# Turning the rows of x and of the softmax shift with DMA transposes in a fused attention kernel

## The reference

```python
xn = _layernorm(x)
# attention on xn
q = (layernorm(xn) * norm_g + norm_b) @ Wq;  k, v = split(xn @ Wkv)
q = q / max(|q|, 1e-12) * q_scale;           k = k / max(|k|, 1e-12) * k_scale
sim  = q @ k.T * 8 - slope[h] * |i - j|      # causal, two null keys ahead
out  = softmax(sim) @ v;                     out = out @ Wout
# result
x + out + ffn(xn)                            # ends in layernorm(...) * ln_g + ln_b
```

## Time and profile before

| | us |
|---|---|
| time, median of 3 runs | 3170.33 |
| lowest, highest | 3167.26, 3171.96 |
| the profiled execution, its own time | 3174.85 |
| its span, first to last instruction | 3173.0 |
| PE busy | 2914.2 |
| DVE busy | 2680.4 |
| ACT busy | 2252.6 |
| POOL busy | 2248.3 |

### The profile page before, as it was taken

The page is one execution under the profiler, slowest core; times in us unless marked ns, Lnnn a source line. Parts: engine busy times, 40 slices in busy tenths (PEclk is TensorE's granted clock), DMA queues, the critical chain, the costliest instruction groups (busy, mean ns, idle before and its releaser), DMA issues.

```text
span 3173.0 us, 86275 instructions
## 1 busy us (share of the span) xinstructions
PE 2914.2 (92%) x32783; PEld 1729.7 (55%) x32783; DVE 2680.4 (84%) x6642; ACT 2252.6 (71%) x3572; POOL 2248.3 (71%) x2588
## 2 busy tenths in 40 slices
PE   4589999899998999989998999989999899998998
PEld 4245555555555556555555555555555555555555
DVE  6778888888888888888888888888888888888887
ACT  3467777676866777767776677766777676867776
POOL 5876677867778577876778668786677867778663
PEclk8799999999999999999999999999999999999999
DMA  3111221212121121211212122121211212221111
GB/s 115 44 25 25 58 42 48 55 22 58 45 64 35 32 58 35 71 28 40 57 40 66 22 50 53 42 58 25 58 42 48 55 22 58 45 64 35 25 25 38
DMA packets 320329, 144.72 MB, mean 46 GB/s; under 512 B 284336, under 2 KB 286384, under 8 KB 319920
## 3 DMA queue, kind: packets, MB, share of 16 engines
q1 hardware_dynamic: 318448, 139.12, 18.5%
q10 hardware_dynamic: 1472, 0.09, 0.0%
HBM read 55.23 MB, written 16.78 MB: 23 GB/s over the span
## 4 chain that ended last, share of the span: by engine, by line
PE 60%; DVE 22%; issue 9%; POOL 7%; ACT 2%; DVEq 0%; POOLq 0%; ACTq 0%
PE PS L1262 8%; PE PS L1237 8%; PE PS L1241 7%; PE PS L1240 7%; DVE PS L1032 7%; PE PS L1285 4%; PE PS L1310 3%; DVE QKB L1047 3%; DVE AR L1070 3%; PE PS L1312 3%; PE PS L1314 3%; PE PS L1331 3%; PE PS L1333 3%; PE PS L1332 3%; PE PS L1266 2%
## 5 line engine op out<-in xcount | busy, mean ns | idle before, releaser
L1032 DVE CUSTOM_DVE_ANT_0 PS<-PS,STR 128x512 f32<-128x512 f32 (+3 forms) x1536 | 825.4, 579 | 192.1 <-PE PS L1285 190.7
L573 ACT ACTIVATE AR<-PS,SC 128x1024 f32<-128x1024 f32 (+1 forms) x640 | 658.5, 1029 | 418.5 <-PE PS L1293 250.0
L1237 PE MATMUL PS<-WH,XT 128*128 128x388 f16 x2048 | 684.4, 334 | 57.7 <-DVE AR L1039 48.4
L799 POOL TENSOR_TENSOR RN<-SS,HALF 128x8 f32<-128x8 f32 x256 | 436.4, 1705 | 417.3 <-DVE SS L1118 412.9
L1240 PE MATMUL PS<-WL,XT 128*128 128x388 f16 x2048 | 684.1, 334 | 0.0
L1241 PE MATMUL PS<-WH,XT 128*128 128x388 f16 x2048 | 683.9, 334 | 0.0
L577 ACT ACTIVATE AR<-AR 128x1024 f16<-128x1024 f32 (+1 forms) x640 | 621.7, 971 | 20.3
L1070 DVE TENSOR_TENSOR AR<-AR 128x768 f16<-128x768 f32 (+1 forms) x448 | 516.3, 1167 | 11.8 <-ACT AR L577 11.8
L1262 PE MATMUL PS<-AR 64*128 64x512 f16 (+3 forms) x4608 | 504.7, 328 | 3.9 <-ACT AR L573 3.8
L1310 PE MATMUL PS<-AR 128*128 128x66 f16 x4608 | 478.0, 193 | 3.9 <-DVE AR L1070 3.8
L1312 PE MATMUL PS<-AR 128*128 128x64 f16 x4608 | 477.7, 195 | 0.0
(11 more groups left out here) (247 smaller groups left out, 5803.6 us busy)
## 6 DMA issues: line engine op xcount, KB each, us to landing
XW<-in_L_attn_x SPq DMA_DIRECT2D x112, 256.0 KB, 2.7
out<-ACC SPq DMA_DIRECT2D x64, 256.0 KB, 2.1
ACC<-in_L_attn_x SPq DMA_DIRECT2D x56, 256.0 KB, 2.7
AR<-QKB SPq DMA_TRANSPOSE x512, 2.5
AR<-in_L_attn_Wkv SPq DMA_DIRECT2D x2, 1536.0 KB, 13.9
ACC<-in_L_attn_x SPq DMA_DIRECT2D x2, 1024.0 KB, 7.1
AR<-in_L_attn_Wout SPq DMA_DIRECT2D x1, 2048.0 KB, 8.4
AR<-in_L_attn_Wq SPq DMA_DIRECT2D x2, 512.0 KB, 5.3
```

Of the source, the lines that this page charges most:

```text
L573: e.activation(PR[:, n % 2, :, 0:wide], SB[:, :, 0:wide], ACT.Exp, scale=SIG).then_inc(s_p, 1)
L799: e.tensor_tensor(RN[:, i % 2, :], SS[:, i % 2, :], HALF[:, :], ALU.pow).then_inc(s_rn, 1)
L1032: e.tensor_tensor_reduce(out=r[:, 0:n], in0=r[:, 0:n], in1=ST[:, u % 2, h, o:o + n], scale=1.0, scalar=LOW, op0=ALU.add, op1=ALU.max, accu ...
L1237: e.matmul(PJ, XT[:, k, xs], WH[:, k, p, :], start=k == 0, stop=False)
```

## The change

1. Rows of x: `ln_tp` on PE and `ln_out` on ACT are gone. SP issues one DMA transpose per row tile, `turn_rows`, from `XHL` straight into `XT`: 128 rows by 1024 numbers. Each of the two slots has its own semaphore. Ahead of the loop the 8 turns of batch 0 stand in SP's queue behind the loads.
2. Rows with the shift: the four turns on PE and the copy on ACT are gone. SP issues one DMA transpose of 128 rows by 512 numbers per half unit.
3. Neither takes a bank of the ring any more.
4. Keys and queries: the factor `KA` is moved into the norm. DVE scales the sum of squares by 1/(KA*KA) in the instruction that takes the larger one, ACT copies without a scale, and DVE makes the low part of a group with one plain subtraction of 128 by 512 instead of two scaled ones of 128 by 256. SP waits for the whole group before it turns either tile.
5. All tables are new.

```diff
-W_PIECE = [45, 46, 50, 56, 62, 66, 71, 74, 78, 82, 84, 90]
-W_SCORE = [90, 94, 98, 104, 108, 113, 118, 122, 126, 132]
+W_PIECE = [45, 46, 48, 57, 64, 66, 70, 74, 77, 82, 84, 91]
+W_SCORE = [91, 94, 100, 105, 108, 114, 118, 122, 126, 132]
...
-W_PROJ = [z for z in [0, 6, 12, 23, 28, 32, 40, 44] for k in range(KC)]
-W_TP = [29, 34, 56, 66]
-W_LO = [26, 38, 48, 61]
-W_SHIFT = [70, 91]
-W_CTP = [75, 96]
-W_CT = [75, 95]
+W_PROJ = [z for z in [-1, 7, 12, 23, 28, 32, 40, 43] for k in range(KC)]
+W_TP = [36, 45, 56, 69]
+W_LO = [27, 39, 56, 65]
+W_SHIFT = [69, 91]
+W_CTP = [75, 99]
...
-W_XL = [-36, -31, -24, -5, 1, 2, 14, 22]
-W_XTP = [-28, -28, -12, -8, 5, 7, 18, 34]
-W_XT = [-30, -28, -13, -10, 5, 13, 19, 38]
+W_XL = [-36, -36, -26, -8, -5, 9, 29, 34]
+W_XTP = [-33, -30, -22, 4, 10, 20, 22, 41]
...
-HOLD = [4.6, 5.2, 6.1, 6.2, 6.8, -39.0, 6.5]
+HOLD = [4.6, 5.2, 7.1, -60.5, 5.5]
...
+            def turn_rows(b, t):
+                w.wait_ge(s_xl, NT * b + t + 1)
+                if b:
+                    w.wait_ge(s_proj, (NP * b - 1) * NT + t + 1)
+                e.dma_start_transpose(XT[:, :, P * t:P * t + P], XHL[:, t % 2, :, :].rearrange("p j c -> p (j c)")).then_inc(s_xt[t % 2], 16)
+            for t in range(NT):
+                turn_rows(0, t)
...
+                for u, qc in due(s, W_CTP):
+                    w.wait_ge(s_c, 2 * u + qc + 1)
+                    w.wait_ge(s_cz, 2 * (2 * u + qc) + 2)
+                    if u > 1:
+                        w.wait_ge(s_st, 2 * NS * (u - 1))
+                    e.dma_start_transpose(CT[:, u % 2, 512 * qc:512 * qc + 512].rearrange("p (q n) -> p q n", q=4),
+                                          CTK[:, qc, :, :].rearrange("p q r -> p (q r)")).then_inc(s_ct[qc], 16)
+                for b, t in due_ln(s, W_XTP):
+                    turn_rows(b, t)
                 for u, g in due(s, W_TP):
...
+                    w.wait_ge(s_lo, i + 1)
                     for t in range(2):
                         c = 256 * g + P * t
-                        w.wait_ge(s_lo, 2 * i + t + 1)
...
-                                 SQ2[:, i % 2, :].rearrange("p (t j c) -> p t j c", t=2, c=64), ACT.Copy, scale=KA).then_inc(s_hi, 1)
+                                 SQ2[:, i % 2, :].rearrange("p (t j c) -> p t j c", t=2, c=64), ACT.Copy).then_inc(s_hi, 1)
...
-                    for t in range(2):
-                        e.scalar_tensor_tensor(
-                            out=QKH[:, i % 3, t, 256:512].rearrange("p (j c) -> p j c", c=64),
-                            in0=SQ2[:, i % 2, 256 * t:256 * t + 256].rearrange("p (j c) -> p j c", c=64), scalar=KA,
-                            in1=QKH[:, i % 3, t, 0:256].rearrange("p (j c) -> p j c", c=64), op0=ALU.mult,
-                            op1=ALU.subtract).then_inc(s_lo, 1)
+                    e.tensor_tensor(QKH[:, i % 3, :, 256:512], SQ2[:, i % 2, :].rearrange("p (t c) -> p t c", t=2),
+                                    QKH[:, i % 3, :, 0:256], ALU.subtract).then_inc(s_lo, 1)
...
-                    e.tensor_tensor(SS[:, i % 2, :], SS[:, i % 2, :],
-                                    CL[:, u // NP % 2, 2 * g:2 * g + 2, :].rearrange("p t c -> p (t c)"), ALU.max).then_inc(s_ss, 1)
+                    e.scalar_tensor_tensor(out=SS[:, i % 2, :], in0=SS[:, i % 2, :], scalar=1.0 / (KA * KA),
+                                           in1=CL[:, u // NP % 2, 2 * g:2 * g + 2, :].rearrange("p t c -> p (t c)"),
+                                           op0=ALU.mult, op1=ALU.max).then_inc(s_ss, 1)
```

More of the change, by code:

```diff
@@ L143, in take @@
         last[i], read[i] = who, slot
-    for t in range(NT):
-        take(t - 600, "xt", 0, t)
     for s in SLOTS:
@@ L152, in ring_order @@
             take(s + HOLD[2], "op", u, t)
[L153 to L156, removed]
         for u, qc in due(s, W_NTP):
-            take(s + HOLD[5], "nt", u, qc)
+            take(s + HOLD[3], "nt", u, qc)
         for u, qc in due(s, W_OTP):
-            take(s + HOLD[6], "otp", u, qc)
+            take(s + HOLD[4], "otp", u, qc)
     return at, before
@@ L343, in bank_free @@
             what, u, i = BEFORE[who]
-            if what == "xt":
-                e.wait_ge(s_xt, NT * u + i + 1)
-            elif what == "s":
+            if what == "s":
                 e.wait_ge(s_mx, 24 * u + i + 1)
@@ L349, in bank_free @@
                 e.wait_ge(s_add, NT * (u // 2) + i + 1)
-            elif what == "ct":
-                e.wait_ge(s_ct, 2 * u + i + 1)
             elif what == "nt":
@@ L542, in _ @@
                     e.activation(QKH[:, i % 3, :, 0:256].rearrange("p t (j c) -> p t j c", c=64),
-                                 SQ2[:, i % 2, :].rearrange("p (t j c) -> p t j c", t=2, c=64), ACT.Copy, scale=KA).then_inc(s_hi, 1)
-                for u, qc in due(s, W_CT):
-                    w.wait_ge(s_ctp, 2 * u + qc + 1)
-                    if u > 1:
-                        w.wait_ge(s_st, 2 * NS * (u - 1))
-                    else:
-                        w.wait_ge(s_spl, 20)
-                    e.activation(CT[:, u % 2, 512 * qc:512 * qc + 512], rb("ct", u, qc).bitcast(F16)[:, 0:512],
-                                 ACT.Copy).then_inc(s_ct, 1)
+                                 SQ2[:, i % 2, :].rearrange("p (t j c) -> p t j c", t=2, c=64), ACT.Copy).then_inc(s_hi, 1)
                 for u, qc in due(s, W_NT):
@@ L1199, in _ @@
                     bias(j // 2)
-            def ln_tp(b, t):
-                r = rb("xt", b, t).bitcast(F16)
-                bank_free(w, "xt", b, t)
-                w.wait_ge(s_xl, NT * b + t + 1)
-                for j in range(8):
-                    ins = e.transpose(r[:, P * j:P * j + P], XHL[:, t % 2, j, :], IDH[:, :])
-                ins.then_inc(s_xtp, 1)
             null_columns(NP - 1)
@@ L1213, in _ @@
             ins.then_inc(s_bqn, 1)
-            for t in range(NT):
-                if t == 6:
-                    w.wait_ge(s_am, 1)
-                    e.transpose(PS[0:8, 2, 192:320], AM[:, 0:8], IDF[:, :]).then_inc(s_amt, 1)
-                    w.wait_ge(s_dg, 1)
-                    e.matmul(PS[:, 2, 320:328], ONE, DG, start=True, stop=True).then_inc(s_amb, 1)
-                ln_tp(0, t)
+            w.wait_ge(s_am, 1)
+            w.wait_ge(s_bqe, 3)
+            e.transpose(PS[0:8, 2, 192:320], AM[:, 0:8], IDF[:, :]).then_inc(s_amt, 1)
+            w.wait_ge(s_dg, 1)
+            e.matmul(PS[:, 2, 320:328], ONE, DG, start=True, stop=True).then_inc(s_amb, 1)
             w.wait_ge(s_ready, 1)
```

102 lines of the change are left out of this document (42 added, 60 removed).

## The result

The changed kernel takes 3036.24 us (median of four runs, 3029.34 to 3043.06) against 3171.14 for the kernel before in the same session: 0.9577 of it, 95% interval 0.9552 to 0.9602.

The account below looks back on a forecast made before the run. The prediction took a nearly full PE stream, with holes that DVE sets, as the bound. Its terms, 43 + 8 + 8 + 24 - 5 = 78 us off 3174.85, gave 3092 us with the median's offset; range 3045 to 3166.

Parts of the forecast that it names:

- part 3: Ring of PSUM banks: 24 of 280 users per batch leave, shortening PE's wait for a bank; 8 us saved (0 to 40).
- the tables: Order of all other work: changes by amounts no row prices; a tenth of the holes is 26 us either way.
- Part 1: PE's stream: 1024 turns leave PE, 54 us of them in the loop; 43 us saved (32 to 54).
- the pace: PE's turns: each further turn costs 0.056 us of PE's stream, so 1024 of them cost 57 us.
- Part 2: ACT: its copies leave, and PE's 8.5 us wait for a bank goes; 8 us saved (0 to 12).
- Part 4: DVE, keys and queries: one 0.89 us subtraction replaces a 1.17 us pair; 24 us saved (7 to 42).
- Part 5: SP's queue: 192 more DMA transposes, 41 us more per batch, latency covered by distances; costed at 5 us.
- the text's own test: PE's waits for DMA in three matmul lines: more than 20 us in all would prove the SP costing wrong.
- SP becomes the bound: SP's in-order queue: shifts or keys held beyond their cover stop PE each half unit; 3220 us, chance 0.11.
- 7.5 us of cover: Shift of a second half: written 10.05 us before first use, less 2.5 us for a landing.
- the 5 us that it found for the keys: Keys held up behind a base load: 5 us of cover left before the piece that reads them.
- More arrives: Whole loop: PE's saving arrives in full and the holes shrink with DVE; below 3060 us, chance 0.14.

Follow-up runs that it names:

- runs 12: Changed kernel where each turned row tile and turned shift again takes a ring bank, held until its DMA has landed; 3178.93 us.
- run 13: Also ring_order_only: changed kernel with the turned row tiles and shifts back in the ring's order as phantoms, but held by nobody; 3147.37 us.
- run 6: All of the new code with the new row tables and every other table from the kernel before; 3190.88 us.
- run 2: Kernel before with only the shift turned by SP's DMA, without PE's turn, ACT's copy or ring banks; 3154.46 us.
- run 1: Also x_rows_only: kernel before with only the x rows turned by SP's DMA, their banks out of the ring, tables unchanged; 3235.08 us.
- run 3: Kernel before with only the scale moved into the norm and the low part made by one subtraction per group; 3160.43 us.
- runs 12 to 15: Besides the two above: changed kernel with turned shifts alone (3139.21 us), then turned row tiles alone (3100.12 us), taking ring banks until landing.
- run 10: Changed kernel with 1024 more turns of 128 by 128 on PE, two ahead of each row tile's product; 3066.47 us.

## Why the prediction was wrong in size

**Two terms failed: the ring's users (part 3), and the tables, which the sum put at nothing.** For the tables it said 26 us either way; with the new code they are worth 215 us (3251 to 3036). Without them the parts together bring nothing: the sum had 78 us for them, and the new code with new row tables alone is 21 us slower than the kernel before, with the old tables 81.

Part 3 priced the users by their share: 9% of a wait of 123.4 us, 11 us, of which 8 were taken, and a third of the wait as the upper end. Put back in the changed kernel, the users cost 111 us without a hold and 143 with one (runs 12 and 13). The fault is in the base as much as in the share. The 123.4 us did not depend on the users: with 24 fewer and only the row tables new they were 123.4 again (run 6), and with the 24 back in the new order they were 30.5 (run 13). What a user does is another thing. The ring has three banks, and `ring_order` gives each user the one that, by the tables and HOLD, has been taken longest; so the tables set not only each engine's order, as the description of the kernel has it, but also who follows whom on a bank. One more user gives the next ones a bank whose last user is more recent. What that costs depends on who that is: here, at one pair of pieces in every second unit, an output product whose addition stands behind others on DVE, 30 waits of 2.4 to 3.8 us. The row of the wait before says nothing on it. These 111 us hold for the new order. With the old tables the shift's 128 users and its turns together gave only 15 us (run 2), so they are no measure of what part 3 brought on the way from the kernel before.

**Part 1, PE's turns:** forecast 43 (32 to 54), measured 30 in the changed kernel. Added to PE, 1024 turns made it busy for 46 us more, near the 57 of the pace; a little over half of 54 us arrives, less than PE's share of the chain.

**Part 2, ACT's copies:** not measured by itself. The wait of 8.5 us in the earlier trace rows is gone; in its place came the wait of ACT for the landing, 12.6 us in the changed kernel and 124.0 in run 1, which this part overlooked.

**Part 4, the low part:** forecast 24 us (7 to 42), measured 9 in the order of before and 16 in the new. The duration was right in the order of before (862 ns against 890), and higher in the denser order (1057 ns, within its 0.68 to 1.09). What failed is that the wait for POOL taken off this instruction was held to be saved. In run 3, where nothing else changed, L1066 took over part of it, 1161 ns after 1041, and DVE lost 36 us where its own group lost 80; in the changed kernel DVE lost 14 us where 72 were expected. The Trainium skill, page "SBUF — State Buffer", section "SBUF: two separate sides", has DVE, with two SBUF inputs, wait for the whole of a POOL operation that reads SBUF and began first. The trace agrees: in the timeline of 1546.73 to 1549.41 the low part ends 0.55 us after POOL's operation.

**Part 5, SP:** forecast 5 us. In the changed kernel the text's own test holds: PE waits 7.4 us for DMA, under the 20 it named. The size of the turn was wrong on the safe side (1.31 us, not 2.6), so SP gets 16 x 1.19 + 8 x 1.31 = 30 us per batch, not 41. But the reasoning looked only at who waits for the turned data, and not at who waits for the slot that the turn reads. That wait is in the changed kernel's ln_hi, where ACT waits for the DMA (s_xt) and no longer for PE (s_xtp), and with the old row tables ACT stood in it for 124.0 us in x_rows_only. Of that kernel's 66 us, 42 went with the wait when the row tables were new (3235 to 3193), in spite of the PE time saved; what makes the other 23 isn't shown, beside 17.5 us for which PE waits for turned rows there. The tables of the rows alone hold 60 to 100 us.

**The rivals.** "SP becomes the bound" was priced at 3220; without the new tables such times are there (3235 and 3251), in part by the slot's way, and with the old row tables in the changed kernel also by its own way (PE waits 78.0 us for keys). What the prediction held against it, 7.5 us of cover, was read for the shift; the 5 us that it found for the keys did not enter the rival's price. "More arrives" was what happened, but not as written: DVE is as busy per batch as before, and PE's busy time fell by more than its turns. That the forecast had the right direction is in part luck, since it rests on parts that gain nothing without the tables which it put at nothing.

**What the measured terms add up to.** In the new order: users 111, turns 30, low part 16, that is 157 us, 22 more than the gain; what stands against them was not measured apart. By the other way, from before: code +81, row tables -60, the other tables -155, in all -134. The two accounts answer different questions; neither leaves a single cause.

**A term that nobody priced: the clock.** The mean granted clock of TensorE was 0.979 before, 0.985 after, 0.971 in ring_order_only and 0.966 in x_rows_only. The records show stretches at 0.5, the lower level of 1.2 GHz: 26 of them in the span before, 12 after, 33 in ring_order_only and 43 in x_rows_only. The pair of L1271 at 1611.53 above is in one, after its hole of 3.74 us: 0.61 us, where pairs of this size take 0.39. Span times (1 - clock) gives 3173.0 x 0.021 = 67 us before, 3041.3 x 0.015 = 46 after and 3148.2 x 0.029 = 91 in ring_order_only. So up to 21 of the 135 us and up to 45 of the 111 us are PE work done at half speed. It is an upper bound, since a slow stretch costs only where PE's work ends last. For ring_order_only the busy times bear it out: 37.6 us more for the same 31759 matmuls. There the phantoms are the only edit, so the lower clock comes from it too, and those 38 us belong to its price. Of the 92.8 us that PE's busy time fell by from before to after, 57 are the turns by their pace, at most 21 the clock, and some 15 stay without an account; a lone turn counts for more than the pace in busy time.

**Open.** How much of the 155 us of the other tables comes from who follows whom on a bank, and how much from the order on the engines, isn't settled: halves of the tables can't be tried apart, and no run has the new tables with the old code. In runs 12 to 15 the order of the ring was the only thing changed, yet the tables were made for a ring without the phantoms; another set made for 280 users might lose less than 111.

## What to carry to other kernels

When an instruction leaves an engine for a DMA, write down three waiters, not one: who reads its result, who reuses what it reads (now held until the landing), and who got the buffer after it. In a ring of few banks a user more or less changes which earlier user the next ones have to wait for; look up in the order who that is and what stands ahead of its reader, instead of scaling the wait that the profile shows. And a change of tables is priced with the code it was made for: the same code gave 3251 us with one set and 3036 with the other.

## What the runs showed of the hardware

- A DMA transpose of 128 rows by 1024 columns of two bytes takes 1.31 us to issue on SP, and one of 512 columns 1.19 to 1.26: the issue hardly depends on the size. The landing goes from 2.4 to 2.9 us after the start. The Trainium skill, page "VectorE: DVE Perf Modes", section "Rules for kernel authors", has TensorE for turns of 128 by 128 where the result may lie in PSUM, and the DMA otherwise. Here the result had to go on to SBUF. In the new order TensorE would not have been better: 1024 turns on PE cost 30 us (run 10), and the profile shows no wait of PE for the new DMA turns. In the order of before it was better for the rows of x (66 us, run 1; 42 of them went with the wait for the slot), and not for the shift (15 us faster by DMA, run 2).
- A subtraction of 128 x 512 from two SBUF inputs takes 0.67 us on DVE at the shortest (L1036 in the changed kernel; the 51 of 256 with no POOL operation beside them have a mean of 0.68), and 1.94 beside a POOL operation of 2.13 us; its mean went from 0.86 to 1.06 us when the order got denser. Work taken off one such operation returned in part as a longer wait in the next: 80 us off one group, 36 off DVE (run 3).
- After a hole of 3.74 us PE worked at a granted clock of 0.5 for a while (the pair at 1611.53), so a hole can cost more than its length. It does not always: of the 30 such pairs in ring_order_only 10 start at 0.5 and 20 at full clock, and two of those 20 come after holes of 3.75 us.
